# A test-time-memory loop on one NeuronCore: one PSUM bank for each pair of images, gradients as four 32-token matmuls, first products by halves

## The reference

```
def _mlp(params, h):
    for w1, w2 in params:              # two layers; w1 is 64x128, w2 is 128x64
        h = h + gelu(h @ w1) @ w2
    return h

def step(carry, x_t):                  # x_t: one image row, 16 tokens of 64 channels, for 8 images
    params, mom = carry
    k = l2norm(x_t @ Wk);  v = x_t @ Wv
    g = grad(mean((_mlp(params, k) - v) ** 2))        # for each image by itself
    new_mom    = eta * mom - lr * g
    new_params = params * (1 - forget) + new_mom
(paramsT, _) = scan(step, 16 rows)
final = mean of paramsT over the 8 images
return _mlp(final, q)
```

## Time and profile before

| | |
|---|---|
| median of 3 runs | 371.03 us (368.09 to 373.56) |
| time of the profiled execution | 373.33 us |
| its span, first to last instruction | 371.2 us |
| mean granted TensorE clock in the span | 0.946 |
| memory loop, first z0 to the end of the last step | 56.03 to 257.90 us |
| TensorE busy in the span | 331.4 us (89%) |
| VectorE busy | 272.0 us (73%) |
| ScalarE, GpSimd busy | 131.2, 143.4 us |

### The profile page before, as it was taken

How to read it: one execution, slowest core, us unless ns; L and a number is a source line. 1 busy time by engine, 2 the same in 40 slices (tenths; PEclk the granted TensorE clock), 3 DMA queues, 4 the chain that set the end, 5 groups by cost and what they waited for, 6 DMA issues and landing times.

```text
span 371.2 us, 7387 instructions
## 1 busy us (share of the span) xinstructions
PE 331.4 (89%) x2656; PEld 235.7 (64%) x2656; DVE 272.0 (73%) x558; ACT 131.2 (35%) x303; POOL 143.4 (39%) x204
## 2 busy tenths in 40 slices
PE   8797999999999999999999999999888575898993
PEld 3343478878877887788788877887333354352852
DVE  0626564677787888678788887887848879969984
ACT  2004653143234433332343224431332174077411
POOL 9000004374657575546465656563000028500001
PEclk9999995698999999789899999999999999699998
DMA  7000000000000000000000000000000000000001
GB/s 315 8 0 2 1 0 2 0 0 0 0 0 0 0 0 0 0 0 0 0 0 0 0 0 0 0 0 0 2 0 1 2 2 1 0 0 2 0 2 57
DMA packets 874, 3.66 MB, mean 10 GB/s; under 512 B 96, under 2 KB 96, under 8 KB 864
## 3 DMA queue, kind: packets, MB, share of 16 engines
q1 hardware_dynamic: 864, 3.52, 2.4%
HBM read 3.00 MB, written 0.52 MB: 9 GB/s over the span
## 4 chain that ended last, share of the span: by engine, by line
PE 71%; DVE 21%; ACT 4%; issue 3%; DVEq 0%; POOL 0%; ACTq 0%; POOLq 0%
PE ps L1103 13%; PE ps L1113 12%; PE ps L1089 8%; PE ps L1098 6%; PE ps L1190 5%; PE ps L1118 4%; PE ps L988 3%; PE ps L1023 2%; PE ps L968 2%; ACT arena_mem L444 2%; PE ps L1334 2%; PE ps L1339 2%; PE ps L1178 2%; DVE arena_att L836 2%; PE ps L1226 2%
## 5 line engine op out<-in xcount | busy, mean ns | idle before, releaser
L320 POOL TENSOR_TENSOR arena_mem<-arena_mem,keep_now 128x512 f32<-128x512 f32 x48 | 49.4, 1042 | 1.3
L968 PE MATMUL ps<-zero 128*128 128x512 bf16 x156 | 41.2, 411 | 4.7 <-DVE uf L856 2.5
L311 POOL COPY k_now<-kbd 128x128 f32 x16 | 4.9, 304 | 86.8 <-PE ps L1077 44.9
L1113 PE MATMUL ps<-arena_mem,u_tok 128*128 128x256 f32 x128 | 38.0, 401 | 0.0
L746 DVE TENSOR_TENSOR arena_mem<-ps,arena_mem 128x512 f32<-128x512 f32 x48 | 33.0, 688 | 5.8 <-PE ps L1113 5.6
L434 ACT ACTIVATE act_u<-ps 128x128 f32<-128x128 f32 x32 | 8.9, 277 | 78.1 <-PE ps L1118 71.6
L705 DVE TENSOR_TENSOR ps<-ps,eta_e 128x512 f32<-128x512 f32 x48 | 33.1, 689 | 0.4 <-PE ps L1077 0.4
L968 PEld LDWEIGHTS ps<-zero 128*128 128x128 bf16 x156 | 15.6, 106 | 27.2 <-issue 9.8
L339 POOL TENSOR_TENSOR arena_mem<-h_tok,spread_now 128x512 f32<-128x512 f32 x16 | 16.6, 1039 | 37.5 <-DVE z_g L730 37.5
L444 ACT ACTIVATE arena_mem<-ps 128x512 f32<-128x512 f32 x48 | 28.7, 597 | 6.5 <-PE ps L1103 4.1
L1103 PE MATMUL ps<-const_sb,arena_mem 128*128 128x128 f32 x192 | 30.7, 285 | 0.0
(11 more groups left out here) (278 smaller groups left out, 706.4 us busy)
## 6 DMA issues: line engine op xcount, KB each, us to landing
const_sb<-const SPq DMA_DIRECT2D x1, 835.5 KB, 5.2
param_sb<-param SPq DMA_DIRECT2D x1, 809.5 KB, 8.1
arena_conv<-band SPq DMA_DIRECT2D x1, 768.0 KB, 6.5
xs_sb<-xs SPq DMA_DIRECT2D x1, 512.0 KB, 3.6
out<-xh SPq DMA_DIRECT2D x2, 256.0 KB, 2.1
```

Of the source, the lines that this page charges most:

```text
L320: pool.tensor_tensor(qe[:, m, :].rearrange("p (b d) -> p b d", b=8), we[:, m, :].rearrange("p (b d) -> p b d", b=8), keep_now[:, 0:8].unsq ...
L968: pe.matmul(ps[:, bank, :], zero_bf[:, 0:P], zero_bf[:, :], start=True, stop=True)
L1113: return pe.matmul(ps[:, m, cols], left, right[:, cols], start=False, stop=False, skip_group_check=True)
```

## The change

1. Momentum is laid out by pairs: bank j (0 to 3) holds the four matrices of pair j, 128 columns each. `momentum(m)` is a view of 4 banks x 128 columns.
2. A gradient is four matmuls, one for each pair: 32 tokens (partitions 32j to 32j+31) of both operands, 128 columns of weights, 128 moving columns, out to bank j. The spread operands, `block_j` and `by_pair` as a spread are gone. The token rows `k_tok`, `h1_tok`, `r_tok` and `dh_tok` are scaled by the learning rate in ScalarE's copy out of PSUM; the last two copies are new.
3. All four gradients stand at the end of the step (w21's just ahead of du0), in the order w21, w11, w20, w10, with one semaphore `grads` behind the last. The three updates of w10, w11 and w20 wait for it. w21's gradient waits until all four momenta are scaled.
4. z0, z1 and du1 are eight matmuls of 64 columns of weights, out to partitions 0 to 63 or 64 to 127, in place of four of 128.
5. On VectorE the scaling of w11's momentum moves from the step's start to just ahead of rbd, that of w10's ahead of dz1, and that of w20's behind dz1.
6. GpSimd copies the next step's k during the present step, so that z0 reads `k_now` at fixed addresses.

```diff
+        def momentum(m):
+            return ps[:, 0:J, m * P:(m + 1) * P]
...
-                def token_rows(out, bank, col, tp, done):
+                def token_rows(out, bank, col, tp, done, scale=1.0):
                     act.wait_ge(sem(tp), t + 1)
-                    act.activation(out, ps[:, bank, col:col + P], ACT.Copy).then_inc(sem(done), 1)
+                    act.activation(out, ps[:, bank, col:col + P], ACT.Copy, scale=scale).then_inc(sem(done), 1)
...
+                token_rows(r_tok[:, :], 7, 2 * P, "r_tp", "r_tok", lr)
                 act.wait_ge(sem("dz1_tp"), t + 1)
...
+                token_rows(dh_tok[:, :], 7, 3 * P, "dh1_tp", "dh_tok", lr)
...
-                updated(3, "g10", "q_10", "w10_new")
-                updated(1, "g11", "q_11", "w11_new")
-                updated(0, "g20", "q_20", "w20_new")
+                updated(3, "q_10", "w10_new")
+                updated(1, "q_11", "w11_new")
+                updated(0, "q_20", "w20_new")
...
-                def per_pair(bank, col, w, x):
+                def per_pair(col, w, x):
                     for j in range(J):
-                        mm = pe.matmul(ps[:, bank, col + 32 * j:col + 32 * j + 32], w[:, P * j:P * j + P],
-                                       x[:, 32 * j:32 * j + 32], start=True, stop=True)
+                        for e in range(2):
+                            mm = pe.matmul(ps[64 * e:64 * e + 64, 4, col + 32 * j:col + 32 * j + 32],
+                                           w[:, P * j + 64 * e:P * j + 64 * e + 64], x(j), start=True, stop=True)
...
-                def gradient(m, left, right, half):
-                    cols = slice(half * BANK // 2, (half + 1) * BANK // 2)
-                    return pe.matmul(ps[:, m, cols], left, right[:, cols], start=False, stop=False, skip_group_check=True)
+                def gradient(m, left, right):
+                    for j in range(J):
+                        tokens = slice(32 * j, 32 * j + 32)
+                        mm = pe.matmul(ps[:, j, m * P:(m + 1) * P], left[tokens, :], right[tokens, :], start=False, stop=False,
+                                       skip_group_check=True)
+                    return mm
...
-                pe.wait_ge(sem("scaled"), 4 * t + 2)
-                pe.wait_ge(sem("r_fbd"), t + 1)
-                gradient(2, u_tok[:, 1, :], r_fbd, 0)
+                pe.wait_ge(sem("scaled"), 4 * t + 4)
+                pe.wait_ge(sem("r_tok"), t + 1)
+                gradient(2, u_tok[:, 1, :], r_tok)
...
+                gradient(1, dz_tok[:, 1, :], h1_tok)
+                pe.wait_ge(sem("dh_tok"), t + 1)
+                gradient(0, u_tok[:, 0, :], dh_tok)
                 pe.wait_ge(sem("dz0_ready"), t + 1)
...
+                gradient(3, k_tok, dz_tok[:, 0, :]).then_inc(sem("grads"), 1)
```

More of the change, by code:

```diff
@@ L304, in _ @@
             pool.wait_ge(sem("coef_ready"), 1)
+            pool.wait_ge(sem("kbd_ready"), 1)
+            pool.tensor_copy(k_now[:, :], kbd[:, 0:P]).then_inc(sem("k_now"), 1)
             with pool.Fori(0, NS) as t:
-                pool.wait_ge(sem("g10"), t + 1)
+                pool.wait_ge(sem("grads"), t + 1)
                 pool.wait_ge(sem("w10_new"), t + 1)
@@ L731, in slope_3, with updated @@
                        .then_inc(sem("slope"), 1)
-                def by_pair(out, col, tp, done, scale):
-                    dve.wait_ge(sem(tp), t + 1)
-                    dve.scalar_tensor_tensor(out[:, :].rearrange("p (j n) -> p j n", j=J),
-                                             ps[:, 7, col:col + P].unsqueeze(1).broadcast_to([P, J, P]), scale,
-                                             cst("block_j").unsqueeze(2).broadcast_to([P, J, P]), ALU.mult, ALU.mult)\
-                       .then_inc(sem(done), 1)
-                def updated(m, grad, q, done):
-                    dve.wait_ge(sem(grad), t + (1 if m < 3 else 2))
-                    dve.wait_ge(sem(q), t + 1)
-                    if m < 3:
-                        dve.tensor_tensor(we[:, m, :], ps[:, m, :], qe[:, m, :], ALU.add).then_inc(sem(done), 1)
-                    else:
-                        dve.tensor_tensor(w10[:, :], ps[:, 3, :], q10[:, :], ALU.add).then_inc(sem(done), 1)
-                mom_scale(1)
+                def updated(m, q, done):
+                    dve.wait_ge(sem("grads"), t + (1 if m == 2 else 2))
+                    dve.wait_ge(sem(q), t + 1)
+                    new, kept = (we[:, m, :], qe[:, m, :]) if m < 3 else (w10[:, :], q10[:, :])
+                    dve.tensor_tensor(by_pair(new), momentum(m), by_pair(kept), ALU.add).then_inc(sem(done), 1)
                 arg(0, "z0_sq", "y0")
@@ L1077, in _ @@
                 pe.matmul(ps[:, m, :], zero_bf[:, 0:P], zero_bf[:, :], start=True, stop=True)\
-                  .then_inc(sem("m_zero" if m < 3 else "g10"), 1)
+                  .then_inc(sem("m_zero" if m < 3 else "grads"), 1)
             pe.wait_ge(sem("v_ready"), 2)
@@ L1108, in turn_weights @@
                     return mm
-                def gradient(m, left, right, half):
-                    cols = slice(half * BANK // 2, (half + 1) * BANK // 2)
-                    return pe.matmul(ps[:, m, cols], left, right[:, cols], start=False, stop=False, skip_group_check=True)
+                def gradient(m, left, right):
[4 more added lines that the diff above has]
+                    return mm
+                pe.wait_ge(sem("k_now"), t + 1)
                 pe.wait_ge(sem("w10_new"), t + 1)
-                for j in range(J):
-                    mm = pe.matmul(ps[:, 4, 32 * j:32 * j + 32], w10[:, P * j:P * j + P], kbd[:, bass.ds(t * P + 32 * j, 32)],
-                                   start=True, stop=True)
-                mm.then_inc(sem("z0_done"), 1)
+                per_pair(0, w10, lambda j: k_now[:, 32 * j:32 * j + 32]).then_inc(sem("z0_done"), 1)
                 pe.wait_ge(sem("w11_new"), t + 1)
@@ L1140, in _ @@
                 pe.wait_ge(sem("h1_ready"), t + 1)
-                per_pair(4, P, wd[:, 1, :], h1bd).then_inc(sem("z1_done"), 1)
+                per_pair(P, wd[:, 1, :], lambda j: h1bd[:, 32 * j:32 * j + 32]).then_inc(sem("z1_done"), 1)
                 pe.wait_ge(sem("u0_tok"), t + 1)
@@ L1160, in _ @@
                 pe.wait_ge(sem("r_ready"), t + 1)
-                per_pair(4, 2 * P, wd[:, 2, :], rbd).then_inc(sem("du1_done"), 1)
+                per_pair(2 * P, wd[:, 2, :], lambda j: rbd[:, 32 * j:32 * j + 32]).then_inc(sem("du1_done"), 1)
                 pe.wait_ge(sem("u1_tok"), t + 1)
```

99 lines of the change are left out of this document (34 added, 65 removed).

## The result

| | before | after |
|---|---|---|
| median of 4 runs each | 372.02 us (368.09 to 373.56) | 424.02 us (423.86 to 425.29) |
| ratio to before | 1 | 1.142 (95% interval 1.133 to 1.152) |
| time of the profiled execution, its span | 373.33, 371.2 us | 424.19, 422.0 us |
| mean granted clock in the span | 0.946 | 0.698 |
| memory loop | 201.9 us | 251.5 us |

A forecast was written before the change was run, and what follows sets the result against it. TensorE was taken to bound the kernel, VectorE close behind. Sixteen steps averaging 13.3 us made a loop of 213 against 202, the profiled 373.33 becoming 384; 383 us was forecast, range 350 to 403.

The forecast's parts named there:

- second rival: Memory loop: TensorE's clock stays at 1.2 GHz throughout, 16 steps of 14.9 us, 408 us in all; chance 0.12.
- the new path: One loop step of the changed kernel at 2.4 GHz, waits included: 10.9 us against 11.8 before.
- Six steps in ten at 14.9 and four at 10.9: Loop's mix of steps at 1.2 and 2.4 GHz: 13.3 us on average, 213 us for sixteen against 202.
- what counts is moving columns, not records: TensorE's clock in the loop: gradients' moving columns hold it; 3.7 us full of them a step become 1.0.
- when w20's, w11's and w10's gradients lie close together: End of a loop step: the clock, expected to fall in nearly every step, comes back only there.
- Two spreads of 1.04 us leave GpSimd, off the path.: GpSimd in each loop step: two spreads of 1.04 us go, taken to lie off the path.
- The price of a step at 1.2 GHz: One changed loop step at the low clock: 12.8 us of TensorE work plus 2.1 of waits, 14.9 us.
- ScalarE's new copies: Two more copies on ScalarE in each loop step, 277 ns each; it stands idle for most of the second half.
- the wait of 0.86 us at the step's start: TensorE ahead of z0: all updates wait for all gradients, so z0 starts 0.86 us after the last gradient.
- the price of a gradient at 2.4 GHz: Each gradient's four matmuls run side by side: 0.24 us each, 1.0 for four against 3.7 before.
- The first rival: Memory loop: the clock stays as it was, loop 182 us, 20 less, 351 us in all; chance 0.27.
- The rule on long idle gaps: TensorE's clock: the skill's page advises only against long idle gaps; no new-path wait exceeds 0.9 us, so the clock would hold.

The follow-up runs named there:

- e5: Changed kernel plus seven matmuls on zeros a step where TensorE waits, and GpSimd waiting for the last slope before multiplying w21: 354.94 us, 0.959 of before.
- e4: Kernel before with its gradients cut to a quarter of their moving columns, three quarters of each left out: 461.5 us.
- e7: Changed kernel with GpSimd's wait for the last slope, momentum scalings moved and w21's gradient later, no added matmuls: 373.56 us (354.76 to 378.74).
- e1: Changed kernel plus seven matmuls on zeros a step, four behind the last gradient and three behind r's transpose: 409.48 us, 1.108 of before.
- e9: Changed kernel with only GpSimd's wait for the last slope put back, ahead of its multiplications of w21 and w10: 427.45 us, 1.152 of before.
- e8: Changed kernel with z0, z1 and du1 whole again, four matmuls of 128 columns of weights each: 459.39 us.
- e6: Changed kernel with six matmuls on zeros a step, GpSimd's wait for the last slope, scalings moved and w21's gradient later: 345.4 us, 0.920 of before.

## Why the prediction was wrong

The case that happened is its second rival, "the clock stays down for the whole loop", given 0.12 and priced at 408; 16 us were missing from its price as well.

**Where the 52 us come from.** With the slopes free and the clock held, the new path is e5's, seven added matmuls included: 11.1 us a step, a loop of 178, or 24 us less than before's 201.9. At 1.2 GHz the steps of after take 15.7, and the loop 251.5: 73.5 us more. The difference is the 49.6 us of the loop.

**The level, the step that failed.** "Six steps in ten at 14.9 and four at 10.9": fifteen steps of sixteen were at the low level throughout, and the first for all but 6.8 us. The argument was right in kind (what counts is moving columns, not records; e4 shows it with nothing else changed), and its own rows could have carried it further. The forecast let the clock come back "when w20's, w11's and w10's gradients lie close together", though it had just priced them at a quarter of the time. In the rows before, the clock rose behind a stretch that held nothing but gradients; after has no such stretch, since at 1.2 GHz its four gradients are 2.5 us together, in two pieces with du0 and a turn between them. That this is why it did not rise is an argument; e7's clock rose with gradients as short. The share of six in ten came from no row.

**GpSimd, the step that was missing.** "Two spreads of 1.04 us leave GpSimd, off the path." What left with them was a wait, and GpSimd's other work moved under VectorE's slopes: 1.4 us a step at full clock (12.5 in e1, 11.1 in e5), and in e1 with it the clock. It is not a part of the 52 us as they stand: e9 has the wait back and nothing else, and takes 427.45 us. The Trainium skill states the rule, on "SBUF — State Buffer", section "Who interferes with whom": VectorE instructions with two SBUF inputs and GpSimd instructions that read SBUF share a read interface, and the later one waits until the earlier has ended. The trace agrees: L717 and L721 with two SBUF inputs went from 0.28 to 0.91 us, L711 with one stayed at 0.27. I had not looked for it, since both engines had time to spare.

**The price of a step at 1.2 GHz**: 14.9 forecast, 15.73 measured. Gradients were put at 0.46 each, 1.8 us; they took 0.53 to 0.74, 2.5 us. The twelve weight turns were put at 2.6 and took 1.04 + 1.00 + 0.99 = 3.0; the eight single turns at 2.0 and took 2.7, 0.26 of it a wait ahead of dh1's product; the six products at 5.8 and took 6.0. That is 2.0 us more. Of the 2.1 us of waits that were forecast, 0.9 at the step's start was left beside that one, since the slower TensorE hides the rest.

What is dearer is mostly a turn *ahead of* a change of mode, and the forecast had priced only the turn behind one. w20's four turns took 0.85 us ahead of the whole du1, and so they do in e8 (153.21 to 154.06), but 0.99 ahead of du1 by halves. The kernel before shows the same in its own steps: w21's four turns, with h2 behind them, took 0.99 at 1.2 GHz (62.53 to 63.52) and 0.53 at 2.4 (102.92 to 103.45), where w20's took 0.43 (104.54 to 104.97). So the price is 0.14 us at 1.2 GHz and 0.10 at 2.4, not 0.05. The turns of z_g and of dh1 fit: 0.35 and 0.40 ahead of a gradient by row groups, 0.21 and 0.27 ahead of one over all rows (69.07 and 70.86 in before). The first gradient's 0.74, ahead of du0, fits too, but no run separates it from the gradients' loads, which end 0.52 us behind the first one's start.

**ScalarE's new copies** were put at 277 ns; with a scale for each partition out of SBUF (`lr_now`) they took 362 to 368. They lie beside other work in after.

**Right**: the wait of 0.86 us at the step's start (0.91); rbd and dz1 right behind a scaling; about the price of a gradient at 2.4 GHz (0.24 forecast, 0.22 to 0.34 in e6, 1.2 us for the four where 1.0 was said); no extra for four banks in scalings and updates; a product by halves (0.59 for 0.58, its end at 0.66 for 0.70); and the path at full clock without GpSimd's interference (11.1 in e5 for 10.9, with the clock kept).

**The first rival**, the clock as it was, was worked out at 351, and e5 took 354.9. It needed seven added matmuls a step and one wait, and that the two numbers agree is in part luck: e5's loop is 178 us for the rival's 182, and what is behind the loop takes 5 us more than before. The rule on long idle gaps, which the prediction cites for that rival, did not decide this case: in the loop of after no wait of TensorE is longer than 1.13 us, and the clock was at 0.50 for 243 us.

## What to carry to other kernels

Before cutting matmul work that is dense in moving columns, look at which stretch of the trace the granted clock rises behind; if it is the one that is cut, price every step at the lower clock, or give the columns back where TensorE waits anyway. When an operation is removed, look for the wait that goes with it, and for what that wait kept apart: here it kept GpSimd from under VectorE's two-input operations. The version with both repaired, e6, beats the kernel before by 8% (0.920, 0.910 to 0.929).

## What was not expected of the hardware

- Less work can take more time: with a quarter of the gradients' columns and all else equal, 461.5 for 372.9 us (e4), at clock 0.50 with TensorE covered by records for 99% of the loop.
- Matmuls on zeros, whose result nobody reads, hold the clock: 0.51 over the loop in e9 and 1.00 in e5, which differ by seven such matmuls a step.
- Both levels hold themselves. In e7 identical steps ran at 10.4 us and then for 71.7 us at 15.3, with no change in the program; e4's loop stood at 0.50 for all of its 285 us, those of e5 and e6 at 1.00 for their 178 and 170.
- In the rows shown the wait between VectorE and GpSimd costs the two unequally: VectorE's operation grows by 0.63 us, GpSimd's by 0.05 (1.04 to 1.09). VectorE's are the short ones here; what a long one ahead of GpSimd's would cost, no run shows.
